# Fewer signals from TensorE, and a tie of POOL's gathers to VectorE's masks, in a graph layer kernel

## The chip, the cores and the metric

One Trainium2 chip, one of its cores. The metric is the device time of one execution in microseconds, lower is better. The engines are TensorE (PE), VectorE (DVE), ScalarE (ACT), GpSimd (POOL) and SyncE (SP), each with its own instruction queue; they are ordered among themselves by counters (semaphores) alone: `then_inc` adds to one when an instruction has ended, `wait_ge` holds an engine until it has a value.

## What is computed

A relational graph layer with attention on 50,000 nodes and 25,000 edges, features 64 wide, 10 relations, `dst` sorted:

```python
proj = jnp.einsum('ni,rio->nro', nfeat, relation_weight)
t_r = proj[src, etype]
h_r = proj[dst, etype]
att = jnp.sum(t_r * jnp.tanh(h_r + efeat), axis=-1)
seg_max = jax.ops.segment_max(att, dst, num_segments=n)
ex = jnp.exp(att - seg_max[dst])
a = ex / jax.ops.segment_sum(ex, dst, num_segments=n)[dst]
h_nb = jax.ops.segment_sum(nfeat[src] * a[:, None], dst, num_segments=n)
out = leaky_relu((nfeat + h_nb) @ res_fc_w.T, 0.01) + leaky_relu(nfeat * h_nb @ res_fc2_w.T, 0.01)
x = _layernorm(x + out)
```

## The kernel before

Edges lie 196 to a partition. They are worked in 25 blocks `s` of 8 columns of 128 edges (the last block has 4). Beside them 49 dense tiles `d` of 1024 nodes get the result for nodes without an edge; blocks -1 to 15 take three tiles each (D0, D1, D2; the last of these blocks only one). The rows of nodes with edges are computed per block and scattered over the dense result at the end.

*POOL* gathers the two end rows of each edge column (`gather`, L443 to L453, 388 indirect DMAs, ring `xsd` of 13 blocks), and then scatters the 196 columns of results (`scatter`, L469 to L477). It runs ahead of the blocks that use the rows, so `pace` (L435 to L441) ties it to the progress of TensorE: `pe_marks` walks TensorE's program and lists, for each signal, how many instructions (a weight load and a matmul are two) TensorE has issued by then. Gather n must wait for the last mark with at most 14.6 n - 250 instructions, scatter n goes on at 13.64 each. An early block has 328 such instructions, a late one 256.

*TensorE*, in each block (L627 to L701): D0's four transposes (`dense_turn`), the edge features into `h_ps` (`add_edges`), scores of the block before (`scores`), D0's product (`dense_y`), then ten quads. A quad is four matmuls (16 instructions in the count of POOL's tie) that add one relation to `t_ps` and `h_ps`. Nine take a mask of VectorE, quad 4 the unmasked copy `xc` of ScalarE. Between the quads stand the steps for block f = s - 2 (two `pair_turn`, behind quads 3 and 4, and four products), D1's turn behind quad 5, D1's product behind quad 6, D2's turn behind quad 7, D2's product behind quad 8; last the transposes of the next block's rows (`turn_in`). Each of these steps ended with a signal. From block f = 14 on (`LATE`) the products are two of one kind (`late_y`) and two of another (`late_linear`).

*ScalarE* copies each turned tile from `tr_ps` to SBUF (`dense_copy` L721, `pair_copy` L785) so that TensorE can go on with it; `tr_ps` is one buffer, so the next turn waits for the copy. It also does the tanh (L710, behind quad 9), the plain copy (L716, behind `turn_in`), relus, squares and the normalised output.

*VectorE* makes the masks `xm` of relation r (`mask`, L989 to L997) in a ring of four, so mask m waits for the quad that read mask m - 4; between the masks it does maxima, sums and layer norm steps. `product` (L1003) needs the tanh, and the next block's mask 0 comes behind it.

*SP* loads node tiles (`load_x`), masks' types (`load_typ`) and edge features (`load_e`, ring of three, freed by `eadd_done`).

## Time and profile before

| | us |
|---|---|
| median of 3 runs | 890.75 |
| lowest, highest of the 3 | 890.29, 2936.04 |
| profiled execution, first to last instruction | 908.0 |
| TensorE busy | 642.8 (71%) |
| VectorE busy | 608.1 (67%) |
| POOL busy | 572.8 (63%) |
| ScalarE busy | 514.2 (57%) |
| granted TensorE clock, mean | 0.844 |

The profiled execution is 17 us longer than the median. Times in the profile are counted from its first instruction. In its rows the bracket behind an instruction gives how long its engine was idle before it and what ended the idle time: "issue" and "remote" mean that no instruction of another engine ended just then.

### The profile page before, as it was taken

The numbers are of one execution on the slowest core, as the hardware profiler recorded it, in microseconds if no ns is written. First come the engines' busy times: TensorE is split into PE (matmuls) and PEld (weight loads), VectorE is DVE, ScalarE is ACT, GpSimd is POOL, SyncE is SP. The second block draws the span as 40 slices with busy tenths as digits, with TensorE's granted clock in tenths as the row PEclk, the third lists the DMA queues.
The fourth block names the chain that finished last, engine by engine and source line by source line (L and its number), as shares of the span: only waits on it lengthen the run. The fifth ranks groups of instructions, "written<-read, shape, count | busy, mean of one in ns | idle before, by whom it ended". The sixth has DMA issues, their size and how long they took to land. (4 is left out here: it accounts for less than half of the span.)

```text
span 908.0 us, 13811 instructions
## 1 busy us (share of the span) xinstructions
PE 642.8 (71%) x3948; PEld 356.0 (39%) x3948; DVE 608.1 (67%) x1094; ACT 514.2 (57%) x1457; POOL 572.8 (63%) x594
## 2 busy tenths in 40 slices
PE   2587778877777877877887876877788778865030
PEld 1434343544443443443443443343344344344020
DVE  2459768778778868869778769865686567754050
ACT  0255575577677667767677677744455244555052
POOL 7466666666666666666666666666666666666726
PEclk9788988798998998999897989879987889786555
DMA  5332432333332432432432421321111110000000
GB/s 139 107 101 71 115 103 81 114 103 81 115 103 81 116 104 69 127 103 67 128 104 60 123 81 45 104 73 64 50 48 43 62 57 28 27 29 28 24 6 17
DMA packets 48035, 70.37 MB, mean 77 GB/s; under 512 B 15971, under 2 KB 19487, under 8 KB 47959
## 3 DMA queue, kind: packets, MB, share of 16 engines
q1 hardware_dynamic: 18562, 32.97, 11.6%
q0 software_dynamic: 18752, 17.29, 9.1%
q10 hardware_dynamic: 10644, 19.23, 5.7%
q8 instruction: 32, 0.52, 0.2%
q14 instruction: 45, 0.36, 0.1%
HBM read 45.60 MB, written 25.78 MB: 79 GB/s over the span
## 5 line engine op out<-in xcount | busy, mean ns | idle before, releaser
L450 POOL DMA_INDIRECT xsd<-in_x,ends_i x388 | 378.4, 975 | 219.4 <-issue 91.1
L558 PE MATMUL t_ps<-xm,w_rel 64*64 64x512 f32 (+1 forms) x900 | 263.1, 682 | 17.7 <-DVE xm L996 9.2
L996 DVE SCALAR_TENSOR_TENSOR xm<-typ,xT_ps 128x1024 f32<-128x1024 f32 (+1 forms) x225 | 264.4, 1185 | 14.6 <-ACT xc L716 9.9
L560 PE MATMUL h_ps<-xm,w_rel 64*64 64x512 f32 (+1 forms) x900 | 264.3, 682 | 0.7 <-issue 0.4
L474 POOL DMA_INDIRECT out<-out_r,row_i x196 | 191.3, 976 | 110.4 <-issue 51.7
L575 PE MATMUL y_ps<-bd_cat,dT 128*128 128x256 f32 x392 | 127.0, 481 | 48.1 <-issue 28.6
L575 PEld LDWEIGHTS y_ps<-bd_cat,dT 128*128 128x128 f32 x392 | 89.3, 239 | 69.6 <-issue 33.8
L558 PEld LDWEIGHTS t_ps<-xm,w_rel 64*64 64x64 f32 x900 | 57.8, 149 | 118.4 <-issue 81.9
L740 ACT ACTIVATE o_t<-zd,rstd 128x64 f32<-128x64 f32 x392 | 98.8, 340 | 0.0
L585 PE MATMUL tr_ps<-ident,uw 128*128 128x128 f32 x196 | 35.9, 312 | 70.3 <-DVE uw L1090 31.9
L1058 DVE TENSOR_TENSOR zd<-rd,y_ps 128x512 f32<-128x512 f32 x49 | 33.4, 681 | 57.5 <-issue 29.8
L585 PEld LDWEIGHTS tr_ps<-ident,uw 128*128 128x128 f32 x196 | 23.3, 155 | 112.0 <-issue 75.9
L785 ACT COPY uwT<-tr_ps 128x512 f32<-128x512 f32 x49 | 28.4, 580 | 67.9 <-PE tr_ps L585 33.6
L1003 DVE TENSOR_TENSOR prod<-t_ps,g_t 128x512 f32<-128x512 f32 (+1 forms) x25 | 17.0, 680 | 71.8 <-issue 42.3
L1038 DVE SCALAR_TENSOR_TENSOR es<-es,wd,wx 128x64 f32<-128x64 f32 x196 | 55.4, 282 | 11.7 <-DVE es L1038 0.5
L595 PEld LDWEIGHTS s_ps<-bd_both,uwT 128*128 128x128 f32 x224 | 32.2, 207 | 75.9 <-issue 70.0
L541 PE MATMUL h_ps<-ident,ea 128*128 128x128 f32 x196 | 31.1, 307 | 41.0 <-issue 24.0
L710 ACT ACTIVATE g_t<-h_ps 128x512 f32<-128x512 f32 (+1 forms) x25 | 14.7, 587 | 80.3 <-remote 77.7
L595 PE MATMUL s_ps<-bd_both,uwT 128*128 128x128 f32 x224 | 43.1, 319 | 23.3 <-issue 23.3
L560 PEld LDWEIGHTS h_ps<-xm,w_rel 64*64 64x64 f32 x900 | 58.0, 149 | 3.5 <-issue 3.5
L726 ACT ACTIVATE rd<-y_ps 128x512 f32<-128x512 f32 x49 | 28.9, 590 | 46.4 <-remote 20.2
L764 ACT ACTIVATE wx<-xsd,wd 128x64 f32<-128x64 f32 x196 | 52.1, 338 | 0.8
(161 smaller groups left out, 982.8 us busy)
## 6 DMA issues: line engine op xcount, KB each, us to landing
x_in<-in_x SPq DMA_DIRECT2D x48, 256.0 KB
typ<-typ_d SPq DMA_DIRECT2D x24, 512.0 KB
out<-o_t ACTq DMA_DIRECT2D x48, 256.0 KB
xsd<-in_x SPq DMA_DIRECT2D x512, 0.2 KB
xsd<-in_x,ends_i POOLq DMA_INDIRECT x388
hist<-es ACTq DMA_DIRECT2D x24, 256.0 KB
ea<-in_edge_attr SPq DMA_DIRECT2D x24, 224.0 KB
out<-out_r,row_i POOLq DMA_INDIRECT x196
```

The costliest lines, as they stand in the source:

```text
L450: pool.indirect_dma_start(xsd[:, s % RX, j, side, :], None, x[:, :], bass.IndirectOffsetOnAxis(ap=ends_i[:, side, c:c + 1], axis=0),).then ...
L474: pool.indirect_dma_start(out[:, :], bass.IndirectOffsetOnAxis(ap=row_i[:, c:c + 1], axis=0), out_r[:, s % RW, j, :], None, bounds_check=t ...
L558: pe.matmul(t_ps[h * D:(h + 1) * D, 0:n], w[0:D, :], moving[0:D, h * n:(h + 1) * n], start=(at == 0), stop=(at == R - 1), skip_group_check ...
L560: mm = pe.matmul(h_ps[(1 - h) * D:(2 - h) * D, 0:n], w[D:P, :], moving[D:P, (1 - h) * n:(2 - h) * n], start=False, stop=(at == R - 1), ski ...
L575: mm = pe.matmul(y_ps[:, j * 2 * P:(j + 1) * 2 * P], dT[:, d % 2, j * P:(j + 1) * P], bd_cat.rearrange("p k f -> p (k f)"), start=True, st ...
L585: mm = pe.transpose(tr_ps[:, j * P:(j + 1) * P], uw[:, g * QUAD + j, :, :].rearrange("p k f -> p (k f)"), ident[:, :])
L595: mm = pe.matmul(s_ps[:, YQ + j * P:YQ + (j + 1) * P], uwT[:, q // 2, k * P:(k + 1) * P], bd_both[:, :], start=True, stop=True)
L740: ins = act.activation(o_t[:, d % RO, j * D:(j + 1) * D], zd[:, d % RZ, j * D:(j + 1) * D], ACT.Copy, scale=rstd[:, s % 2, d % 3, j:j + 1])
L764: ins = act.activation(wx[:, j, :], xsd[:, e % RX, j, 0, :], ACT.Copy, scale=wd[:, e % 2, 0, j:j + 1])
L996: v.scalar_tensor_tensor(xm[:, m % RM, 0:n], typ[:, s % RT, 0:n], float(r), xT_ps[:, 0:n], ALU.is_equal, ALU.mult).then_inc(masked, 1)
L1038: v.scalar_tensor_tensor(es[:, e % RS, j, :], old, wd[:, e % 2, 1, j:j + 1], wx[:, j, :], ALU.mult, ALU.add).then_inc(chain_done, 1)
L1058: v.tensor_tensor(zd[:, d % RZ, :].rearrange("p (j f) -> p j f", j=4), rd[:, d % 2, :].rearrange("p (j f) -> p j f", j=4), y_ps.rearrange( ...
```

## The change

TensorE no longer signals behind the edge features, behind quads 0, 2, 3, 5, 6 and 8, nor behind the first of two products of a kind in a late block. All who waited for these wait for the next signal that is left: masks for quads 1, 4, 7 or 9, the edge load for quad 1. `quads_until(s, at)` gives the count of quad signals that says that quad `at` of block s is done. `pe_marks` is replaced by `mask_marks`: the tie of POOL now reads `masked`, VectorE's count of masks; mask r of a block stands for (r + 1)/9 of the block's TensorE instructions. The constants of the tie stay.

```diff
+    POSTS = [1, PLAIN_AT, 7, R - 1]
+
+    def quads_until(s, at):
+        return len(POSTS) * s + sum(1 for n in POSTS if n < at) + 1
+
+    def mask_read(m):
+        return quads_until(m // RB, m % RB + (1 if m % RB >= PLAIN_AT else 0))
+
+    Q_BEFORE = [0]
+    for s in range(NS):
+        Q_BEFORE.append(Q_BEFORE[-1] + (2 * groups(s) if s < LATE else 2))
...
+        def mask_marks():
+
+            marks, work, ends = [], 0, {}
             for s in range(-1, LAST + 1):
                 main, e, f, d = 0 <= s < NS, s - 1, s - 2, tiles(s)
+                other = 24 * len(d) + (2 * cols(e) if 0 <= e < NS else 0) + (24 * groups(f) if 0 <= f < NS else 0)
+                if main:
+                    other += 2 * cols(s) + R * 16
+                if 0 <= s + 1 < NS:
+                    other += 2 * cols(s + 1)
+                for r in range(RB):
                     if main:
+                        marks.append((masked, s * RB + r + 1, work + other * (r + 1) // RB))
+                work += other
+                ends[s] = work
             return marks, ends
...
-                wait(sp, eadd_done, s - RE + 1)
+                wait(sp, quad_done, quads_until(s - RE, 0) if s >= RE else 0)
...
-            (marks, ends), at = pe_marks(), [-1]
+            (marks, ends), at = mask_marks(), [-1]
...
-                mm.then_inc(eadd_done, 1)
...
-                mm.then_inc(quad_done, 1)
+                if at in POSTS:
+                    mm.then_inc(quad_done, 1)
... (late_y and late_linear alike)
-                mm.then_inc(y12_done, 1)
+                if g == groups(f) - 1:
+                    mm.then_inc(y12_done, 1)
...
-                act.wait_ge(quad_done, (e + 1) * R)
+                act.wait_ge(quad_done, quads_until(e, R - 1))
...
-                wait(act, quad_done, (s - 1) * R + PLAIN_AT + 1 if s > 0 else 0)
+                wait(act, quad_done, quads_until(s - 1, PLAIN_AT) if s > 0 else 0)
...
-                wait(v, quad_done, quad_count(m - RM) if m >= RM else 0)
+                wait(v, quad_done, mask_read(m - RM) if m >= RM else 0)
...
-                v.wait_ge(y12_done, Q_BEFORE[f] + groups(f))
+                v.wait_ge(y12_done, Q_BEFORE[f] + 1)
```

## Rows read from the trace of the kernel before

**Rows 1.** The page, part 1: busy us (share of the span) xinstructions

```profile
PE 642.8 (71%) x3948; PEld 356.0 (39%) x3948; DVE 608.1 (67%) x1094; ACT 514.2 (57%) x1457; POOL 572.8 (63%) x594
```

**Rows 2.** Stretches: us, busy us of PE, PEld, DVE, ACT, POOL, clock, DMA

```profile
50.00:600.00 550.00, 428.79 (x2628) 236.63 (x2620) 423.13 (x720) 373.72 (x1087) 349.16 (x359) 0.89 0.34 97
600.00:825.00 225.00, 174.79 (x1136) 89.85 (x1136) 145.87 (x264) 98.77 (x272) 144.75 (x149) 0.84 0.13 44
825.00:908.00 83.00, 16.43 (x74) 14.29 (x74) 19.78 (x60) 31.42 (x83) 48.75 (x50) 0.52 0.06 19
```

**Rows 3.** Instruction groups of POOL: busy us, mean ns, idle before them

```profile
L450 POOL DMA_INDIRECT xsd<-in_x,ends_i x388 | 378.4, 975 | 219.4 <-issue 91.1 <-remote 69.4 <-PE h_ps L560 26.3
...
L474 POOL DMA_INDIRECT out<-out_r,row_i x196 | 191.3, 976 | 110.4 <-issue 51.7 <-remote 29.2 <-ACT out_r L810 15.6
```

**Rows 4.** Waits over the span: us in total, times, longest

```profile
ACT g_t L710 <- remote: 77.7, 13, 10.4
```

**Rows 5.** Timeline of POOL, block 11: start us, us, instruction, idle before

```profile
421.99 0.95 POOL L450 DMA_INDIRECT xsd<-in_x,ends_i  x1 [1.35 <-remote]
...
429.48 0.95 POOL L450 DMA_INDIRECT xsd<-in_x,ends_i  x1 [1.54 <-remote]
```

**Rows 6.** Timeline of ScalarE, block 11

```profile
421.82 0.59 ACT L785 COPY uwT<-tr_ps 128x512 f32<-128x512 f32 x1 [0.72 <-remote]
...
423.27 0.57 ACT L785 COPY uwT<-tr_ps 128x512 f32<-128x512 f32 x1
...
429.25 0.59 ACT L721 COPY dT<-tr_ps 128x512 f32<-128x512 f32 x1 [2.00 <-remote]
...
441.57 0.60 ACT L710 ACTIVATE g_t<-h_ps 128x512 f32<-128x512 f32 x1 [1.81 <-remote]
```

**Rows 7.** Timeline of TensorE, block 11

```profile
417.98 0.66 PE L585 MATMUL tr_ps<-ident,uw 128*128 128x128 f32 x4 [0.22 <-issue]
...
425.76 1.06 PE L568 MATMUL tr_ps<-ident,x_in 128*128 128x128 f32 x4
...
429.88 1.99 PE L575 MATMUL y_ps<-bd_cat,dT 128*128 128x256 f32 x8 [1.38 <-ACT dT L721]
```

**Rows 8.** Timeline of VectorE, block 11 (L996: masks; L1058: dense add)

```profile
411.73 2.34 DVE L996 SCALAR_TENSOR_TENSOR xm<-typ,xT_ps 128x1024 f32<-128x1024 f32 x2
...
429.11 1.21 DVE L996 SCALAR_TENSOR_TENSOR xm<-typ,xT_ps 128x1024 f32<-128x1024 f32 x1
433.88 0.69 DVE L1058 TENSOR_TENSOR zd<-rd,y_ps 128x512 f32<-128x512 f32 x1 [3.56 <-ACT rd L726]
...
445.91 2.34 DVE L996 SCALAR_TENSOR_TENSOR xm<-typ,xT_ps 128x1024 f32<-128x1024 f32 x2
```

**Rows 9.** Timelines of TensorE, POOL and ScalarE, the kernel's start

```profile
24.09 0.60 PE L568 MATMUL tr_ps<-ident,x_in 128*128 128x128 f32 x4
...
27.89 0.95 POOL L450 DMA_INDIRECT xsd<-in_x,ends_i  x1 [0.31 <-issue]
...
32.66 0.59 ACT L721 COPY dT<-tr_ps 128x512 f32<-128x512 f32 x1 [5.33 <-remote]
```

**Rows 10.** Timelines of TensorE, POOL and VectorE, the tail

```profile
832.33 3.62 PE L606 MATMUL y_ps<-bd_relu,uwT 128*128 128x128 f32 x16
...
837.20 1.00 PE L613 MATMUL tr_ps<-bd_lin,uwT 128*128 128x64 f32 x8
...
825.55 0.97 POOL L474 DMA_INDIRECT out<-out_r,row_i  x1 [1.68 <-remote]
...
861.40 0.97 POOL L474 DMA_INDIRECT out<-out_r,row_i  x1 [0.31 <-issue]
877.98 0.97 POOL L474 DMA_INDIRECT out<-out_r,row_i  x1 [15.61 <-ACT out_r L810]
...
844.05 0.69 DVE L1111 SCALAR_TENSOR_TENSOR zf<-y_ps,xsd 128x512 f32<-128x512 f32 x1 [6.16 <-remote]
...
866.60 0.69 DVE L1122 TENSOR_TENSOR zf<-zf,tr_ps 128x512 f32<-128x512 f32 x1 [21.13 <-remote]
```

More of the change, by code:

```diff
@@ L64, in gnn_resnorm @@
         G_BEFORE.append(G_BEFORE[-1] + groups(s))
-    Q_BEFORE = [2 * n for n in G_BEFORE]
     C_BEFORE = [QUAD * n for n in G_BEFORE]
@@ L82, in gnn_resnorm @@
     PLAIN_AT = 4
-    def quad_count(m):
-        return m // RB * R + m % RB + (2 if m % RB >= PLAIN_AT else 1)
+    POSTS = [1, PLAIN_AT, 7, R - 1]
[3 more added lines that the diff above has]
+        return quads_until(m // RB, m % RB + (1 if m % RB >= PLAIN_AT else 0))
     LATE = (ND - 1) // 3 - 2
+    Q_BEFORE = [0]
+    for s in range(NS):
+        Q_BEFORE.append(Q_BEFORE[-1] + (2 * groups(s) if s < LATE else 2))
     ROW_BLOCKS = [8, 13, 19, 24]
@@ L214, in gnn_resnorm @@
         scattered = sems("scattered", RW)
-        xT_done, masked, quad_done, eadd_done = sem("xT_done"), sem("masked"), sem("quad_done"), sem("eadd_done")
+        xT_done, masked, quad_done = sem("xT_done"), sem("masked"), sem("quad_done")
         tanh_done, prod_done, att_done, max_done = sem("tanh_done"), sem("prod_done"), sem("att_done"), sem("max_done")
@@ L540, in add_edges @@
                 for i in range(half):
-                    mm = pe.matmul(h_ps[:, i * P:(i + 1) * P], ea[:, s % RE, 2 * i:2 * i + 2, :].rearrange("p h f -> p (h f)"),
+                    pe.matmul(h_ps[:, i * P:(i + 1) * P], ea[:, s % RE, 2 * i:2 * i + 2, :].rearrange("p h f -> p (h f)"),
                                    ident[:, :], start=(i == 0), stop=False, skip_group_check=True)
-                mm.then_inc(eadd_done, 1)
             def quad(s, at):
@@ L613, in late_linear @@
                     mm = pe.matmul(tr_ps[:, j * D:(j + 1) * D], uwT[:, g, k * P:(k + 1) * P], bd_lin[:, :], start=True, stop=True)
-                mm.then_inc(y12_done, 1)
+                if g == groups(f) - 1:
+                    mm.then_inc(y12_done, 1)
             def pair_part(f, q):
```

46 lines of the change are left out of this document (removed).

## The prediction

> **What bounds the kernel now.** I read the page first: the span, the busy times, the two big groups of POOL. No engine is full: over the span TensorE, the busiest, is busy 71% [rows 1]. The stretch table says where: from 50 to 600 us TensorE has 428.8 us of work in 550, from 600 to 825 us 174.8 in 225, and from 825 us on almost none, at half clock [rows 2]. So in 25 blocks TensorE waits about a fifth of the time, and then there is a tail. I looked for the waits by name next. The costliest idle with an unseen cause is ScalarE's ahead of the tanh: 77.7 us in 13 cases, put down to "remote" [rows 4]. The tanh waits for one TensorE signal, that of quad 9.
>
> Then one block (s = 11) in time, engine by engine, signal against waiter. The first pair turn ends at 417.98 + 0.66 = 418.64; its copy on ScalarE starts at 421.82, 3.2 us later, 0.72 us of it with ScalarE idle [rows 7, 6]. D1's turn ends at 425.76 + 1.06 = 426.82; its copy starts at 429.25, 2.4 us later, after 2.00 us of idle [rows 7, 6]. Yet the second pair turn, which can't begin before the first copy ends at 421.82 + 0.59 = 422.41, is copied at 423.27: at once [rows 6]. What differs is POOL. Its indirect DMAs come back to back, 0.30 us apart, in runs of four to six, with breaks of 1.35 and 1.54 us that end at 421.99 and 429.48: 0.17 and 0.23 us behind the two late copies [rows 5, 6]. So POOL, which also waits for TensorE's signals, got them at the same moment. My reading is that a TensorE signal sent inside a run is read when the run has stopped.
>
> The two places where a run is long bear this out. At the start POOL issues 20 gathers in a row, the last at 27.89. D1's first turn ends at 24.09 + 0.60 = 24.69 and is copied at 32.66: 8.0 us late, 3.8 us after POOL fell still at 27.89 + 0.95 [rows 9]. In the tail 29 indirect DMAs run from 825.55 to 862.37. The relu products end at 832.33 + 3.62 = 835.95 and VectorE takes them at 844.05, 8.1 us late; the linear ones end at 838.20 and are taken at 866.60, 28.4 us late, 4.2 us after POOL's last [rows 10]. So what bounds the kernel is the chain of TensorE and ScalarE steps, stretched by TensorE signals that wait out POOL's runs, and at the end 20 scatters of 1.28 us from 877.98 on, behind that chain [rows 3, 10].
>
> The Trainium skill, page "Perfetto Trace Analysis", section "Per-engine timelines", says that the end of a matmul in a profile is an estimate of the profiler and the signal comes after the write is acknowledged. This case agrees that lateness of tenths may be the estimate; 8.0 and 28.4 us can't be.
>
> **The change part by part.** *Signals.* An early block (three dense tiles) signals 25 times: ten quads, one each for edges, scores and x turns, six for the dense tiles, two pair turns, four products. Six quads and the edges go: 18. A late block goes from 19 to 10. No matmul gets shorter or starts sooner by itself, so I cost the removal at 0 on TensorE. What it may save is queueing in front of the signals that matter, which is the rival below.
>
> *Coarser waits.* Masks 4, 6 and 8 now wait for quads 1, 4 and 7 in place of 0, 2 and 5. Quads 1 and 4 are long done. Mask 8 started at 429.11 [rows 8], while quad 7 comes behind D1's product, 429.88 + 1.99 = 431.87, and takes about 1 us: the mask starts some 4 us later and ends at about 434.2 [rows 7, 8]. Queued behind it on VectorE is D1's add, which ScalarE's relu held until 433.88 anyway [rows 8]; it slips by 0.3 us, and by as much as quad 7's signal is late. TensorE needs it only for D2's product, behind quad 8 and two more products. I cost it at 0 and keep 1 us a block as its bound. The edge load now waits for quad 1 of a block two back: 0. The plain copy and the tanh wait for the same quads as before.
>
> *The tie.* This is the part with weight. Before, POOL's gather n waits for TensorE's work to reach 14.6 n - 250 instructions, in 20-odd marks a block, and those marks are themselves the signals that come late: the tie stops POOL after some five gathers, and the stop lets the signals out. Now the marks are the nine masks. An early block is 72 + 16 + 48 + 176 + 16 = 328 instructions, so a mask frees 36.4/14.6 = 2.5 gathers and a block 22.5. One gather costs 0.95 + 0.30 = 1.25 us [rows 3, 5], so 2.5 of them 3.1 us. The masks start at 411.73 to 429.11, eight steps in 17.4 us (2.2 us each) [rows 8]: faster than POOL works them off. So POOL will run from mask 0 without a stop: masks 0 to 5 need only quad 1, and free 15 gathers, 18.8 us; all nine are 28 us. Then it rests until the next mask 0 (445.91, so this period is 34.2 us [rows 8]). A late block is 256 instructions: 18.8 scatters of 1.28 us, 24 us out of 28.
>
> What sits inside the run: the two pair turns and D1's turn, each of which TensorE must get back through a ScalarE copy. Each is now late by 0 to 3.2 us, about 2.8 where it is late. Inside a long run the rows give 8.0 and 8.1 us. So the step per signal is bounded by -2.8 (prompt) and +5.2 (as in the long runs). I take +1.6, nearer to the steady rows: the first of the three still falls in the first 6 us of the run. Early block: 3 x 1.6 = +4.8. At the boundary POOL rests, so quad 9's signal comes sooner; of the 1.81 us idle before the tanh [rows 6] I give back 1.2, as the end of a 28 us run and the 4 us behind it reach to +32. Net +3.6, times 16 = +58 us. Late block: two signals, +3.2, nothing at the boundary, since a run of 24 us fills it; times 9 = +29 us.
>
> *Head.* Masks start only with block 0, and the first frees gather 25 or 26: (88 + 29 + 250)/14.6 = 25.1. POOL issues 26 gathers in place of 20 before it stops, 6 x 1.25 = +7.5 us, and D1's turn, which waits out that run, is as much later. *Tail.* The last mask is done before the last quads, so POOL starts its last run earlier, and three signals stand in it in place of five. The waits there are 6.16 and 21.13 us [rows 10]; the run's length doesn't change, only its start, by some 6 scatters: -8 us.
>
> Sum: 58 + 29 + 7.5 - 8 = +86 on the profiled 908.0 us: 994 us. The median of the runs is 890.75, 0.981 of the profiled execution; 994 x 0.981 = **975 us**.
>
> **Rivals.** (1) *Fewer signals, faster.* If TensorE's signals leave one by one through gaps in a run, those that matter pass sooner when 7 of 25 others are gone, and the boundary, where tanh, plain copy and scores hang one behind the other, falls into POOL's rest. For it: not every signal is late, as the second pair turn shows [rows 6]. Against: that one came 1.2 us into a run (421.99), not deep in one [rows 5]. Price: 1.8 us in each of 25 blocks, 45 us, head and tail cancelling: 863, as a median 846; with 28% off each of three late signals (0.8 us x 3 x 16 = 38 us more) 810. It decides if the second pair turn is copied within 3 us inside a run of more than ten. Chance 0.30, some of it (0.03) too small to tell.
> (2) *No effect.* The lateness may hang on something else than POOL's run length, and the tie still sets POOL's mean rate of 22.5 gathers a block: same period, 891 us. Against: both long runs. Chance 0.13. The Trainium skill, page "VectorE: DVE Perf Modes", section "The DRAIN you can't avoid", measured that a semaphore behind each of eight copies costs nothing over one behind the last; carried to TensorE it gives this rival's time. The trace agrees as far as TensorE's own work goes, and disagrees for the waiters.
> (3) *Full starvation.* The signals wait out the whole run. Then the second pair copy comes 18.8 + 4 = 22.8 us after mask 0's end in place of 10.3 (423.27 against 411.73 + 1.2): 12.5 x 16 = 200, and half of it in 9 late blocks, 56: 908 + 256 = 1164 profiled, 1142. Against: masks 6 and 8 hang on quads 4 and 7, so POOL starves itself sooner. Chance 0.10.
> My forecast has 0.47, with 915 to 1050 as its own range.
>
> **Numbers.** A measurement of this kernel can tell 2% from no change. Faster by more: 0.27, from (1). Within 2%: 0.17, from (2), 0.03 of (1) and the low end of mine. Slower: 0.56. The range of 830 to 1060 leaves out the far part of (1), about 0.09, and (3) with the top of mine, about 0.11.
>
> **What would show it.** In the profile after: POOL in runs of 15 or more from mask 0, then a rest of 5 us or more ahead of the next mask 0; the second pair copy over 10 us behind mask 0; periods of 36 to 40 us for 34.2; the tanh's idle shorter. Runs of POOL still of five would show the tie wrong; long runs with prompt copies would show (1). The head's copy at about 40 us in place of 32.66 tests the mechanism by itself. The prediction fails if lateness falls with the number of signals more than it grows with the run.

## The result and the profile after

| | us |
|---|---|
| changed kernel, median of 4 runs | 1091.24 (1080.38 to 1094.78) |
| kernel before, median | 890.79 |
| ratio, 95% interval | 1.2233, 1.2178 to 1.2288 |
| profiled execution of the changed kernel, first to last instruction | 1078.7 (before: 908.0) |

The change costs 22%. Slower was the forecast, but 975 us was far too low, and the range to 1060 us did not hold the time.

The work itself is the same. Part 1 of the page (busy us, share of the span, instructions) of the changed kernel, against [rows 1]:

```profile
PE 649.4 (60%) x3948; PEld 351.7 (33%) x3948; DVE 607.9 (56%) x1094; ACT 515.0 (48%) x1457; POOL 577.5 (54%) x594
```

TensorE is busy 6.6 us longer (649.4 against 642.8; its mean granted clock was 0.785 against 0.844) and no other engine by more than 5 us; nearly all of the 170.7 us between the two spans is waiting. Where it was lost shows in the start of a block's mask 0. Timelines of VectorE, first of the kernel before and then of the changed one, masks 0 of blocks 0, 16 and 24 (a row can hold several masks):

```profile
42.67 3.48 DVE L996 SCALAR_TENSOR_TENSOR xm<-typ,xT_ps 128x1024 f32<-128x1024 f32 x3
...
577.30 2.35 DVE L996 SCALAR_TENSOR_TENSOR xm<-typ,xT_ps 128x1024 f32<-128x1024 f32 x2 [1.13 <-ACT xc L716]
...
801.45 1.28 DVE L996 SCALAR_TENSOR_TENSOR xm<-typ,xT_ps 128x512 f32<-128x512 f32 x2
```

```profile
50.13 3.48 DVE L964 SCALAR_TENSOR_TENSOR xm<-typ,xT_ps 128x1024 f32<-128x1024 f32 x3
...
725.86 2.34 DVE L964 SCALAR_TENSOR_TENSOR xm<-typ,xT_ps 128x1024 f32<-128x1024 f32 x2
...
983.19 1.28 DVE L964 SCALAR_TENSOR_TENSOR xm<-typ,xT_ps 128x512 f32<-128x512 f32 x2 [0.16 <-ACT xc L684]
```

| part | before | after | difference | forecast |
|---|---|---|---|---|
| head, to mask 0 of block 0 | 42.7 | 50.1 | +7.5 | +7.5 |
| 16 early blocks | 534.6 | 675.7 | +141.1 | +58 |
| 8 of the late blocks | 224.2 | 257.3 | +33.2 | +29 for nine |
| last block and tail | 106.6 | 95.5 | -11.0 | -8 |

Half of the loss stands in the forecast; what is missing is nearly all in the early blocks. The waits of the changed kernel (us in total, times, longest) name it. In the kernel before the longest entry with an unseen cause was the tanh's 77.7 us [rows 4]; now it is the copy of the pair turns, then the masks that wait for TensorE, and POOL, which waits for masks:

```profile
ACT uwT L753 <- remote: 264.6, 37, 13.3
POOL xsd L416 <- DVE xm L964: 258.1, 63, 15.8
DVE xm L964 <- remote: 180.8, 25, 10.9
```

One early block of the changed kernel (s = 9), timelines of POOL, TensorE, ScalarE and VectorE. L416 are the gathers, L525 the last matmul of quad 4, L551 the pair turns, L753 their copies, L678 the tanh, L964 the masks:

```profile
431.47 0.94 POOL L416 DMA_INDIRECT xsd<-in_x,ends_i  x1 [5.16 <-DVE xm L964]
...
451.66 0.94 POOL L416 DMA_INDIRECT xsd<-in_x,ends_i  x1 [0.30 <-issue]
458.52 1.24 POOL L416 DMA_INDIRECT xsd<-in_x,ends_i  x1 [5.91 <-DVE xm L964]
...
464.41 1.35 POOL L416 DMA_INDIRECT xsd<-in_x,ends_i  x1 [0.31 <-issue]
473.04 0.94 POOL L416 DMA_INDIRECT xsd<-in_x,ends_i  x1 [7.29 <-DVE xm L964]
...
437.29 0.59 PE L525 MATMUL h_ps<-xc,w_rel 64*64 64x512 f32 x1
439.94 0.63 PE L551 MATMUL tr_ps<-ident,uw 128*128 128x128 f32 x4 [2.06 <-issue]
...
439.23 0.56 ACT L753 COPY uwT<-tr_ps 128x512 f32<-128x512 f32 x1
...
454.06 0.58 ACT L753 COPY uwT<-tr_ps 128x512 f32<-128x512 f32 x1 [13.30 <-remote]
...
467.19 0.59 ACT L678 ACTIVATE g_t<-h_ps 128x512 f32<-128x512 f32 x1
...
429.99 2.34 DVE L964 SCALAR_TENSOR_TENSOR xm<-typ,xT_ps 128x1024 f32<-128x1024 f32 x2
...
447.09 1.22 DVE L964 SCALAR_TENSOR_TENSOR xm<-typ,xT_ps 128x1024 f32<-128x1024 f32 x1 [4.51 <-remote]
...
471.56 2.34 DVE L964 SCALAR_TENSOR_TENSOR xm<-typ,xT_ps 128x1024 f32<-128x1024 f32 x2
```

POOL issues 17 gathers back to back from 431.47 to 452.60, rests 5.91 us, does five more by 465.76 and rests 7.29 us. The second pair turn ends at 440.57 and is copied at 454.06, 13.5 us late, 1.5 us after the run's end. Mask 0 ended at about 431.2, so the copy comes 22.9 us behind it, where it came 10.3 us behind it in block 11 of the kernel before. From this copy to the tanh it takes 13.1 us where it took 18.3 (423.27 to 441.57, [rows 6]). 12.6 lost, 5.2 given back: this is the 7.4 us by which the period is longer (471.56 - 429.99 = 41.6; 34.2 in block 11 before).

The first pair turn, 5.4 us into the run, was not held (its copy at 439.23 waited only for ScalarE); quad 4 ends at 437.88 (it signals), and the mask that needs it starts at 447.09, 9.2 us later but 5.5 us before the run ends. So a held signal can come out inside a run. In block 3 it is the first pair turn's. Its two copies and POOL's last gather of the run that began at 175.93:

```profile
189.45 0.58 ACT L753 COPY uwT<-tr_ps 128x512 f32<-128x512 f32 x1 [7.56 <-remote]
...
197.25 0.59 ACT L753 COPY uwT<-tr_ps 128x512 f32<-128x512 f32 x1 [6.26 <-remote]
...
193.63 0.94 POOL L416 DMA_INDIRECT xsd<-in_x,ends_i  x1 [0.30 <-issue]
```

The first turn ends at 181.74 and is copied 7.7 us later, inside the run; the second can only then begin, ends at 191.26 and is copied 6.0 us later, 2.7 us after the run's end. Over blocks 2 to 15 the second copy comes 21.3 us behind mask 0's end (11.5 before), and from there to the next mask 0 it takes 20.1 us (21.4 before): 9.8 us lost, 1.3 given back. The 5.2 us of blocks 9 and 11 are not typical.

Head and tail of the changed kernel: POOL, ScalarE (L689: copy of a dense tile) and VectorE (L1079: takes the relu products):

```profile
34.88 0.94 POOL L416 DMA_INDIRECT xsd<-in_x,ends_i  x1 [0.30 <-issue]
51.62 0.94 POOL L416 DMA_INDIRECT xsd<-in_x,ends_i  x1 [15.81 <-DVE xm L964]
...
40.15 0.58 ACT L689 COPY dT<-tr_ps 128x512 f32<-128x512 f32 x1 [5.71 <-remote]
...
1029.47 0.97 POOL L440 DMA_INDIRECT out<-out_r,row_i  x1 [0.30 <-issue]
...
1033.39 0.69 DVE L1079 SCALAR_TENSOR_TENSOR zf<-y_ps,xsd 128x512 f32<-128x512 f32 x1 [6.72 <-remote]
```

26 gathers in place of 20, and D1's first copy at 40.15 in place of 32.66 [rows 9], 7.5 us later: as forecast. In the tail a run of 20 scatters (1005 to 1030, ahead of the last scatters, which start at 1037) holds the relu products until 1033.39, and the wait of 21.13 us behind them [rows 10] is gone.

### The profile page after: what moved, and what is told of

The parts are those of the page before. It is cut to its first block and busy times, and to the rows that moved or that the text cites. A ratio compares the mean times of both kernels' runs of the same rounds, so it can differ in the third digit from the quotient of the medians.

```text
span 1078.7 us, 13797 instructions
## 1 busy us (share of the span) xinstructions
PE 649.4 (60%) x3948; PEld 351.7 (33%) x3948; DVE 607.9 (56%) x1094; ACT 515.0 (48%) x1457; POOL 577.5 (54%) x594
## 5 line engine op out<-in xcount | busy, mean ns | idle before, releaser
L416 POOL DMA_INDIRECT xsd<-in_x,ends_i x388 | 382.6, 986 | 363.3 <-DVE xm L964 258.1
L964 DVE SCALAR_TENSOR_TENSOR xm<-typ,xT_ps 128x1024 f32<-128x1024 f32 (+1 forms) x225 | 264.5, 1186 | 285.8 <-remote 180.8
L523 PE MATMUL t_ps<-xm,w_rel 64*64 64x512 f32 (+1 forms) x900 | 276.6, 704 | 18.0 <-DVE xm L964 14.5
L525 PE MATMUL h_ps<-xm,w_rel 64*64 64x512 f32 (+1 forms) x900 | 276.6, 704 | 0.0
L753 ACT COPY uwT<-tr_ps 128x512 f32<-128x512 f32 x49 | 28.6, 583 | 269.8 <-remote 264.6
L541 PE MATMUL y_ps<-bd_cat,dT 128*128 128x256 f32 x392 | 113.1, 440 | 62.3 <-ACT dT L689 49.2
L551 PE MATMUL tr_ps<-ident,uw 128*128 128x128 f32 x196 | 41.0, 346 | 148.6 <-issue 105.5
L541 PEld LDWEIGHTS y_ps<-bd_cat,dT 128*128 128x128 f32 x392 | 83.5, 224 | 80.0 <-ACT dT L689 55.8
L534 PE MATMUL tr_ps<-ident,x_in 128*128 128x128 f32 x196 | 36.6, 319 | 105.4 <-issue 61.9
L551 PEld LDWEIGHTS tr_ps<-ident,uw 128*128 128x128 f32 x196 | 26.6, 172 | 188.8 <-issue 169.1
L561 PE MATMUL s_ps<-bd_both,uwT 128*128 128x128 f32 x224 | 49.3, 354 | 28.4 <-issue 28.4
L534 PEld LDWEIGHTS tr_ps<-ident,x_in 128*128 128x128 f32 x196 | 26.7, 164 | 112.1 <-issue 111.8
L1006 DVE SCALAR_TENSOR_TENSOR es<-es,wd,wx 128x64 f32<-128x64 f32 x196 | 55.1, 281 | 12.5 <-ACT wx L732 1.3
L1048 DVE RECIPROCAL rstd<-sd 128x32 f32<-128x32 f32 x29 | 10.2, 352 | 77.4 <-ACT sd L765 49.2
L525 PEld LDWEIGHTS h_ps<-xm,w_rel 64*64 64x64 f32 x900 | 53.0, 149 | 0.0
L778 ACT ACTIVATE out_r<-zcf,rstd 128x64 f32<-128x64 f32 x196 | 49.1, 333 | 0.0
L689 ACT COPY dT<-tr_ps 128x512 f32<-128x512 f32 x49 | 28.8, 588 | 39.6 <-remote 36.8
```

What stands on the lines that cost most here:

```text
L416: pool.indirect_dma_start(xsd[:, s % RX, j, side, :], None, x[:, :], bass.IndirectOffsetOnAxis(ap=ends_i[:, side, c:c + 1], axis=0),).then ...
L523: pe.matmul(t_ps[h * D:(h + 1) * D, 0:n], w[0:D, :], moving[0:D, h * n:(h + 1) * n], start=(at == 0), stop=(at == R - 1), skip_group_check ...
L525: mm = pe.matmul(h_ps[(1 - h) * D:(2 - h) * D, 0:n], w[D:P, :], moving[D:P, (1 - h) * n:(2 - h) * n], start=False, stop=(at == R - 1), ski ...
L534: mm = pe.transpose(tr_ps[:, j * P:(j + 1) * P], x_in[:, d % RI, j * P:(j + 1) * P], ident[:, :])
L541: mm = pe.matmul(y_ps[:, j * 2 * P:(j + 1) * 2 * P], dT[:, d % 2, j * P:(j + 1) * P], bd_cat.rearrange("p k f -> p (k f)"), start=True, st ...
L551: mm = pe.transpose(tr_ps[:, j * P:(j + 1) * P], uw[:, g * QUAD + j, :, :].rearrange("p k f -> p (k f)"), ident[:, :])
```

## The experiments

The theory: a signal of TensorE that is sent while POOL issues indirect DMAs back to back is read when the run has stopped (by block 3 above that can't be the whole rule); the mask tie makes the runs long; the fewer signals and the coarser waits cost nothing. Rivals: the coarser waits or the missing signals bring the loss; the number of signals matters; POOL's run has nothing to do with it.

### One part of the change alone, and the first surprise

tie_only has all signals of the kernel before and the new tie; signals_only the reverse; mask_tie_pair_stops is the changed kernel with two more stops of POOL; head_26 is the kernel before with a longer first run.

```diff
tie_only, against the kernel before:
-            (marks, ends), at = pe_marks(), [-1]
+            (marks, ends), at = mask_marks(), [-1]
signals_only, against the changed kernel (pe_marks without the signals that are gone):
-            (marks, ends), at = mask_marks(), [-1]
+            (marks, ends), at = pe_marks(), [-1]
mask_tie_pair_stops, in mask_marks (and POOL waits for every mark that it passes):
+                        if r == 2 and 0 <= f < NS:
+                            marks.append((tr_out, TR_PAIR[f, 0] + 1, work + other * (r + 1) // RB))
+                        if r == 3 and 0 <= f < NS:
+                            marks.append((tr_out, TR_PAIR[f, 1] + 1, work + other * (r + 1) // RB))
head_26, in pace of the kernel before:
+                if n < 26:
+                    return
```

tie_only:


> All of TensorE's signals as in the kernel before; only POOL's tie is the new one (it reads VectorE's masks). Theory (a TensorE signal sent while POOL issues indirect DMAs back to back is read when the run stops, and the tie makes the runs long): nearly the whole loss is here, 1050 to 1110 us, POOL in runs of 15 gathers from mask 0, second pair copy about 22 us behind mask 0. If the loss came from the signals taken away or from the coarser mask waits: 880 to 905 us.

signals_only:


> The signals taken away and the coarser waits as in the changed kernel; POOL's tie still reads TensorE, by the marks that are left (12 to 15 a block in place of 25). Theory: the runs of POOL grow little, so little is lost: 885 to 915 us, late waits of 2 to 4 us as before. If fewer signals or the coarser waits were the cause of the loss: above 1000 us. If fewer signals help (my rival 1 of the prediction): 810 to 875 us.

mask_tie_pair_stops:


> The changed kernel, but POOL also stops within its run, at the third mask for ScalarE's copy of the block's first pair turn and at the fourth for that of its second. Nothing else differs. Theory: each stop lets TensorE's signal out, so both pair copies come within 4 us of the turn, the second 10 to 14 us behind mask 0 in place of 20 to 23, and most of the 141 us lost in the early blocks comes back: 930 to 990 us. If long runs in themselves (or the tie's rate, or coarser mask waits) are the cause: 1060 us or more, since an added wait of POOL can only delay it.

head_26:


> The kernel before; only POOL's first 26 gathers are free of the tie, in place of 20. Theory: ScalarE's copy of the second dense tile, which waits out the first run, comes 6 x 1.25 = 7.5 us later, and block 0's first mask too: 898 us, 0.8% above before. If the copy waits for something else than POOL's run: 891 us, copy at 32.7 us as before.

Measured: 765.85, 764.60, 765.34 and 765.25 us, beside a kernel before of **766.05 us** (31 runs, 762.57 to 767.64). Ratios 0.9996 [0.9978, 1.0013], 0.9990 [0.9975, 1.0005], 1.0001 [0.9985, 1.0017], 0.9992 [0.9971, 1.0014]. Every number of these expectations was missed, because the kernel before itself was 125 us faster than at first (890.79). The page of tie_only, its two groups of POOL (busy us, mean ns, idle before them), and two rows of POOL's timeline:

```profile
L408 POOL DMA_INDIRECT xsd<-in_x,ends_i x388 | 383.6, 989 | 119.2 <-issue 108.0
...
L432 POOL DMA_INDIRECT out<-out_r,row_i x196 | 193.5, 987 | 59.7 <-issue 58.8
...
405.67 0.99 POOL L408 DMA_INDIRECT xsd<-in_x,ends_i  x1 [0.30 <-issue]
406.96 0.95 POOL L408 DMA_INDIRECT xsd<-in_x,ends_i  x1 [0.30 <-issue]
```

POOL issues its 584 indirect DMAs without one pause over 0.6 us from the first to the last: 383.6 + 119.2 + 193.5 + 59.7 = 756 of 764.4 us. Here TensorE's signals are read at once in the middle of an endless run: the second pair copy starts within 0.2 us of its turn in every block. So the sum of my prediction rests on a condition that is not always there. Without it POOL is the bound, the tie never stops it, and neither part of the change matters.

### Is it the program, or the condition it runs in?

after_again is the changed kernel, before_again the one before, both unedited; head_26_again is head_26. more_signals is the kernel before with two signals more behind each quad's inner matmuls:

```diff
                 for h in range(2):
                     pe.matmul(t_ps[h * D:(h + 1) * D, 0:n], w[0:D, :], moving[0:D, h * n:(h + 1) * n],
-                              start=(at == 0), stop=(at == R - 1), skip_group_check=True)
+                              start=(at == 0), stop=(at == R - 1), skip_group_check=True).then_inc(extra, 1)
```

after_again:


> The changed kernel as it is, measured again, because four variants and the kernel before itself all took 765 us together where the kernel before had taken 891 earlier. Two readings: (a) what made TensorE's signals late is no part of the program but of the chip or its condition, and where the kernel before takes 766 us the changed kernel takes 760 to 775 too, bound by POOL's 584 indirect DMAs of 1.25 us (730 us) back to back; where the kernel before takes 890, the changed one takes 1080 to 1095. (b) The change itself brings the lateness in any condition: 950 us or more beside a kernel before of 766.

before_again:


> The kernel before, for a profile of it beside the others. Reading (a): about 766 us, POOL without breaks from 3.5 us on, D1's first copy at about 25 us in place of 32.7; if the late signals are back, 891 us and 32.7 us.

head_26_again:


> The kernel before with the first 26 gathers free, once more. If signals are late here: about 898 us, D1's first copy at about 40 us. If they are prompt: 766 us, copy at about 25 us.

more_signals:


> The kernel before with two more signals of TensorE behind each quad's inner matmuls, which nobody reads (20 more a block, 45 in place of 25). If signals are late here and they leave one by one through gaps (my rival 1): each of the three late signals of a block has up to twice as many ahead, 3 x 1.6 x 25 = 120 us more, about 1000. If they all leave when POOL's run stops: within 1% of the kernel before. If signals are prompt: equal to the kernel before, 766 us.

Measured, together: kernel before 900.79 us (13 runs, 896.18 to 912.49), after_again 1071.61, ratio 1.1879 [1.1777, 1.1981]; before_again 898.75; head_26_again 914.09; more_signals 909.24, ratio 1.0058 [1.0011, 1.0105]. The late signals were back, and reading (a) holds: the same programs come in two conditions (the changed kernel a little under the 1080 to 1095 that I had expected). The whole series:

| measured together | record's chip number | kernel before |
|---|---|---|
| tie_only, signals_only, mask_tie_pair_stops, head_26 | 8 | 766 |
| after_again, before_again, head_26_again, more_signals | 2 | 901, late |
| tie_only_2, signals_only_2, pair_stops_2, tie_handoffs | 9 | 765 |
| probes_mixed; all_mixed | 5; 13 | 763; 768 |
| all_mixed_b | 2 | 763 |
| all_mixed_c | 9 | 910, late |
| loaded_probes; loaded_probes_b | 8; 14 | 766; 765 |

Numbers 2 and 9 show both, so it isn't fixed to a chip's number; inside one group it never changed. The profile tells which it is by the span of the kernel before and by POOL's runs.

The head tests the mechanism. Timelines of ScalarE, before_again and then head_26_again with POOL's last gather of the first run (ScalarE: L726 and L728 D0's relu, L721 and L723 the copy of D1; both kernels' turn of D1 ends at 25.1):

```profile
30.39 0.60 ACT L726 ACTIVATE rd<-y_ps 128x512 f32<-128x512 f32 x1 [9.98 <-remote]
31.15 0.59 ACT L721 COPY dT<-tr_ps 128x512 f32<-128x512 f32 x1 [0.16 <-remote]
```

```profile
30.46 0.60 ACT L728 ACTIVATE rd<-y_ps 128x512 f32<-128x512 f32 x1 [10.03 <-remote]
38.86 0.59 ACT L723 COPY dT<-tr_ps 128x512 f32<-128x512 f32 x1 [7.80 <-remote]
...
35.59 0.94 POOL L452 DMA_INDIRECT xsd<-in_x,ends_i  x1 [0.30 <-issue]
```

Nothing but POOL's tie differs, seven gathers more (26 against 19 in before_again) move D1's copy by 7.7 us, and 914.09 is 1.7% above 898.75 (one run of each; I had said 0.8%). The time by itself proves little: the slowest of the 13 runs of the kernel before took 912.49. But the relu, whose product ended at about 24.3, starts at 30.4 in both, in head_26_again 6 us before the run ends. So "read when the run has stopped" is not exact: inside a run a held signal can still come out, here some 6 us late; only the next one waited for the run's end. The first profile of the kernel before had this too: there the same product ends at 24.26 and its relu starts at 26.73, inside the run that ends at 28.84. Twenty more signals a block (more_signals) cost 0.6%, so a queue of signals has little weight while runs are short: that is against my rival 1.

The traces also record each rise of a counter, and there the signal itself is late, not its reading: the turns' counter in block 9 above rises at 454.04, 0.02 us ahead of the copy. Counted over the changed kernel's first profile, with a run as indirect DMAs less than 0.6 us apart, TensorE's counters rise within 0.4 us of the matmul's end for 74 of the 89 signals in the first 3 us of a run, 11 of 53 from 3 to 6 us, 5 of 73 later in a run, and 157 of 168 outside of runs. Some 20 of these 383 signals have no record at all, too few to explain it. In tie_only, with POOL in one endless run, it is 571 of 578.

### The same experiments again, and a tie on the hand-overs

tie_handoffs has the changed kernel's signals, and its marks are ScalarE's copies and relus, the masks, the tanh and the plain copy, each at TensorE's place in the program:

```diff
+                def turned(k):
+                    if len(d) > k:
+                        mark(tr_out, TR_DENSE[d[k]] + 1, 8)
+                def multiplied(k):
+                    if len(d) > k:
+                        mark(relu_done, d[k] + 1, 16)
```

tie_only_2:


> Again all of TensorE's signals and only the tie new, since one chip reads signals promptly and others late. Where the kernel before takes about 890 to 900 us: theory (long runs of POOL's indirect DMAs hold the signals) 1040 to 1110 us, runs of 15 from mask 0; signals or coarser mask waits as the cause: 885 to 915. Where the kernel before takes 766: 766.

signals_only_2:


> Again the fewer signals and coarser waits with POOL's tie on TensorE. Where the kernel before takes about 890 to 900 us: theory 885 to 930 (the marks that are left are farther apart, so runs grow a little, the head's from 20 to 26 as in the changed kernel); fewer signals as a gain: 810 to 875; coarser waits or fewer signals as the loss: above 1000. Where the kernel before takes 766: 766.

pair_stops_2:


> Again the changed kernel with two more stops in POOL's run, for ScalarE's copies of the two pair turns. Where the kernel before takes about 890 to 900 us and the changed one 1070 to 1090: theory, a stop lets the signals out, both copies within 4 us of their turns and 100 us or more won back, 930 to 990; if a stop of POOL doesn't matter, 1060 or more. Where the kernel before takes 766: 766.

tie_handoffs:


> The changed kernel's fewer signals, but POOL's tie reads the answers to TensorE's signals instead of masks alone: ScalarE's copies of each turned tile, its relus, its tanh and plain copy, and the masks, each at TensorE's place in the program. POOL so stops until each hand-over has been taken, in 20-odd marks a block. Theory: every late signal finds POOL at rest soon after it is sent, 860 to 900 us where the kernel before takes 890 to 900. If the stops cost POOL more than they give (its 584 DMAs need 730 us of any span): 920 or more. Where the kernel before takes 766: 766 to 775.

Measured: kernel before 764.98, and 764.53, 763.49, 762.55, 764.51 us; ratios 0.9991 [0.9978, 1.0003], 0.9981 [0.9971, 0.9991], 0.9974 [0.9961, 0.9987], 0.9989 [0.9977, 1.0000]. No late signals, so only the last sentence of each expectation was put to the test, and it held. The 0.2 and 0.3% of fewer signals did not show in the first series (0.9990, 1.0001): I make nothing of them.

### Every treatment in one execution

Because a whole kernel may meet the wrong condition, the next kernels change their treatment from block to block, and stand behind small probes of the signal itself. A probe is eight rounds between a sender and an answerer beside one kind of work on POOL.

```diff
+            lists = [f() for f in (pe_marks, mask_marks, stop_marks, act_marks)]
+            for s in range(-1, LAST + 1):
+                kind = next((k for a, b, k in kinds if a <= s <= b), 0)
+                marks += [m[:3] for m in lists[kind][0] if m[3] == s]
...
+    def posts(s):
+        return range(R) if s in FULL else POSTS
... (TensorE's side of a probe)
+                        wait(engine, pong, m)
+                        engine.transpose(tr_ps[:, 0:P], ident[:, :], ident[:, :]).then_inc(ping, 1)
... (ScalarE's side)
+                        engine.wait_ge(ping, m + 1)
+                        engine.copy(dT[:, 0, 0:P], tr_ps[:, 0:P]).then_inc(pong, 1)
```

probes_mixed:


> Ahead of the kernel stand seven probes, and then the kernel before runs (all of TensorE's signals) with POOL's tie by blocks: on TensorE's marks to block 4 and from block 17, on the masks in blocks 5 to 10, on the masks with the two stops for the pair copies in blocks 11 to 16. A probe: a sender does one small operation and signals, an answerer copies and signals back, eight times, while POOL (1) rests, (2, 3, 4, 7) issues 16 gathers of 1.25 us, (5) does 16 memsets, (6) issues 16 direct DMAs. Senders and answerers: TensorE and ScalarE in 1, 2, 5, 6 and 7 (7: each gather waits for the one before to land), VectorE and ScalarE in 3, TensorE and VectorE in 4. On a chip where the kernel before takes about 890 us I expect: 1 and 3 in under 8 us; 2 and 4 not done before the run of gathers is (over 20 us); 5 as 1; 6 not known, 7 at the gathers' own pace, about 2 us a round. If TensorE's signals are late for another reason, 2 is as fast as 1. The blocks: before's period of some 33 us in blocks 1 to 4, 40 to 43 in 6 to 10 if the long run is the cause (33 if not), 33 to 37 in 12 to 16 if stops let signals out. On a chip where the kernel before takes 766 us: all probes under 10 us (7 too), and all blocks equal at about 27 us.

all_mixed:


> The same seven probes, and behind them a kernel whose blocks differ. Blocks 1 to 5: all of TensorE's quad signals, POOL's tie on the masks. Blocks 6 to 9: the changed kernel's fewer signals and coarser waits, tie on TensorE's marks that are left. Blocks 10 to 12: fewer signals, tie on the masks, with the two stops for the pair copies. Blocks 13 to 16 and 21 to 24: fewer signals, tie on the hand-overs (ScalarE's copies and relus, masks). Blocks 17 to 20: as 6 to 9. On a chip with late signals I expect: probes 1 and 3 in under 8 us, 2 and 4 not before POOL's run ends (over 20 us), 5 as 1; blocks 2 to 5 at 40 to 44 us (the tie is the cause; about 34 if the signals were), blocks 7 to 9 at 33 to 36 (about 42 if fewer signals or coarser waits were), blocks 11 and 12 at 33 to 37, blocks 14 to 16 at 31 to 34. On a chip where the kernel before takes 766 us: the seven probes as fast as one another and all early blocks at about 27 us.

all_mixed_b:


> The kernel whose blocks differ, once more (blocks 1 to 5: all quad signals, tie on the masks; 6 to 9 and 17 to 20: fewer signals, tie on TensorE's marks; 10 to 12: fewer signals, tie on the masks with the two stops; 13 to 16 and 21 to 24: fewer signals, tie on the hand-overs), behind nine probes: the seven of before, and two more of TensorE and ScalarE in which POOL issues 16 gathers in fours, resting behind each four until they have landed (8), or doing two memsets of 0.47 us behind each four (9). On a chip with late signals: probes 1 and 3 under 8 us, 2 and 4 not before POOL's run ends (over 20 us), 5 as 1, 8 one to three rounds in each rest, 9 like 8 if it is the issue of DMAs that holds the signals and like 2 if it is POOL being busy. Blocks 2 to 5 at 40 to 44 us, 7 to 9 at 33 to 36, 11 and 12 at 33 to 37, 14 to 16 at 31 to 34. On a chip where the kernel before takes 766 us: all probes alike and all early blocks at about 27 us, as two runs have shown.

all_mixed_c:


> The same kernel as the last, on whichever chip it meets. With late signals (kernel before about 890 us): probes 1 and 3 under 8 us, 2 and 4 over 20 us, 5 as 1; blocks 2 to 5 at 40 to 44 us, 7 to 9 at 33 to 36, 11 and 12 at 33 to 37, 14 to 16 at 31 to 34. Without: probes alike, early blocks about 27 us.

probes_mixed, all_mixed and all_mixed_b met no late signals: spans of 918.7, 920.5 and 966.2 us with the probes in them, and for instance all of all_mixed's periods from block 2 to block 14 between 27.3 and 28.6 us, whatever the treatment. all_mixed_c met them (kernel before 909.96, this kernel 1218.01).

*The blocks.* VectorE's timeline of all_mixed_c, masks 0 of blocks 2, 6, 10, 11 and 13, and below it those of blocks 2 and 6 in before_again and in after_again:

```profile
312.18 2.34 DVE L1199 SCALAR_TENSOR_TENSOR xm<-typ,xT_ps 128x1024 f32<-128x1024 f32 x2
...
494.61 2.34 DVE L1199 SCALAR_TENSOR_TENSOR xm<-typ,xT_ps 128x1024 f32<-128x1024 f32 x2
...
631.61 2.34 DVE L1199 SCALAR_TENSOR_TENSOR xm<-typ,xT_ps 128x1024 f32<-128x1024 f32 x2
...
682.46 2.34 DVE L1199 SCALAR_TENSOR_TENSOR xm<-typ,xT_ps 128x1024 f32<-128x1024 f32 x2
...
768.84 2.34 DVE L1199 SCALAR_TENSOR_TENSOR xm<-typ,xT_ps 128x1024 f32<-128x1024 f32 x2
```

```profile
98.46 2.34 DVE L996 SCALAR_TENSOR_TENSOR xm<-typ,xT_ps 128x1024 f32<-128x1024 f32 x2
...
236.26 2.34 DVE L996 SCALAR_TENSOR_TENSOR xm<-typ,xT_ps 128x1024 f32<-128x1024 f32 x2
```

```profile
125.01 2.34 DVE L964 SCALAR_TENSOR_TENSOR xm<-typ,xT_ps 128x1024 f32<-128x1024 f32 x2
...
300.48 2.34 DVE L964 SCALAR_TENSOR_TENSOR xm<-typ,xT_ps 128x1024 f32<-128x1024 f32 x2
```

| blocks of all_mixed_c | signals, tie | period | same blocks, kernel before | same blocks, changed kernel |
|---|---|---|---|---|
| 2 to 5 | all of the quads, masks | 45.6 | 34.5 | 43.9 |
| 6 to 9 | fewer, TensorE | 34.3 | 34.0 | 41.5 |
| 11, 12 | fewer, masks with stops | 43.2 | 35.2 | 43.0 |
| 14 to 16 | fewer, hand-overs | 34.4 | 30.3 | 36.5 |
| 17 to 20 | fewer, TensorE | 28.9 | 27.6 | 32.8 |
| 21 to 23 | fewer, hand-overs | 30.4 | 28.1 | 31.7 |

(Periods in us, each the distance between two mask-0 rows over the number of blocks; the two right-hand columns from before_again and after_again. I had expected 40 to 44, 33 to 36, 33 to 37 and 31 to 34 in the first four rows.) The tie alone brings the whole loss of an early block, 11.1 us, and a bit more than the changed kernel's 9.4. The fewer signals with their coarser waits cost 0.3 us in early blocks and 1.3 us in late ones, inside what one block differs from another (32.7 to 35.9 us in blocks 6 to 9). Both halves of my theory on the change stand, in the one execution that could test them. The hand-over tie is no gain: 2 to 4 us a block behind the kernel before.

The stops are a miss: 33 to 37 us expected, 43.2 measured, though they did what they should. ScalarE's timeline of all_mixed_c, block 11, with POOL's two runs (L987 pair copy, L992 takes a pair product, L928 D1's relu):

```profile
691.71 0.56 ACT L987 COPY uwT<-tr_ps 128x512 f32<-128x512 f32 x1
...
693.14 0.56 ACT L987 COPY uwT<-tr_ps 128x512 f32<-128x512 f32 x1
...
704.48 0.37 ACT L992 COPY l<-s_ps 128x256 f32<-128x256 f32 x1 [4.97 <-remote]
...
714.44 0.60 ACT L928 ACTIVATE rd<-y_ps 128x512 f32<-128x512 f32 x1 [8.37 <-remote]
...
693.04 0.94 POOL L620 DMA_INDIRECT xsd<-in_x,ends_i  x1 [2.35 <-ACT uwT L987]
...
710.50 0.94 POOL L620 DMA_INDIRECT xsd<-in_x,ends_i  x1 [0.30 <-issue]
716.52 0.95 POOL L620 DMA_INDIRECT xsd<-in_x,ends_i  x1 [5.08 <-DVE xm L1199]
```

The second pair copy comes at 693.14, 0.1 us behind its turn. Then POOL makes up for the stop with 15 gathers in a row, and the stall moves to the next signals: the second product of the pairs (ended at 697.89, taken at 704.48, inside the run) and D1's product, ended at 699.65 and read at 714.44, 14.8 us late and 3.0 us after the run's end. What counts is not which signal a stop serves, but how long the run behind it is.

*The probes.* One round of probe 2 in all_mixed_c, beside POOL's run (L463 TensorE's transpose, L471 ScalarE's copy, L643 the gathers):

```profile
31.46 0.47 PE L463 MATMUL tr_ps<-ident 128*128 128x128 f32 x1 [0.35 <-ACT dT L471]
31.97 0.27 ACT L471 COPY dT<-tr_ps 128x128 f32<-128x128 f32 x1 [0.56 <-issue]
32.13 0.94 POOL L643 DMA_INDIRECT out_r<-in_x,ends_i  x1 [0.30 <-issue]
```

I expected over 20 us for the eight rounds of probes 2 and 4. The eighth copy starts 6.4 and 6.6 us in, a round each 0.83 us, in the same execution whose blocks lose 10 us each to late signals. So a run of gathers alone does not hold TensorE's signals in its first 6.4 us, though in the kernel most are held from about 3 us on (11 of 53 in time, above). Every probe was prompt, which leaves the probes unable to tell gathers from memsets or direct DMAs.

### Longer and loaded probes

A round here may hold eight matmuls like those of two quads, probes run beside 24 gathers (30 us), and VectorE and SP can be given work.

```diff
+        PROBES = [(0, 0, ""), (24, 0, ""), (0, 2, ""), (24, 2, ""), (24, 0, "v"), (24, 0, "sp"), (24, 2, "v sp"), (4, 2, ""),
+                  (24, 2, "signals"), (24, 2, "v sp signals")]
+        ROUNDS, OPS, LOADS = [26, 26, 10, 10, 26, 26, 10, 10, 10, 10], 30, 12
```

loaded_probes (the first eight of them):


> On a chip with late signals the first probes came out prompt, which fells the simple form of my theory: eight rounds between TensorE and ScalarE took 6.4 us beside a run of gathers, as without one. They covered only the first 6.4 us of the run, and nothing else ran. Here eight probes, ahead of the kernel with fewer signals and the tie on TensorE (signals_only). A round: TensorE (optionally after eight matmuls like those of two quads) transposes and signals, ScalarE copies and signals back. (1) 26 rounds, POOL at rest; (2) 26 rounds beside 24 gathers in one run; (3) 10 loaded rounds, POOL at rest; (4) 10 loaded rounds beside the run; (5) as 2 with VectorE adding without a pause; (6) as 2 with 12 direct DMAs of 256 KB issued by SP; (7) as 4 with both; (8) as 4, POOL resting behind every four gathers. On a chip with late signals: theory A (the run fills something after some 3 us, whatever else goes on) 2 to 7 all stall until the run ends, 30 us; theory B (it takes traffic of other DMAs beside the gathers) only 6 and 7; theory C (it takes TensorE's own load) 4 and 7, and 8 in part; theory D (VectorE's load) 5 and 7. The kernel behind: blocks as in the kernel before, within 1 us of its periods. Without late signals: 2, 5 and 6 as 1, and 4, 7 and 8 as 3.

loaded_probes_b:


> The eight probes of the last run and two more: (9) as 4, with four more signals of TensorE in each round that nobody reads; (10) as 7, with those signals too. On a chip with late signals: theory A (length of the run alone) 2 and 4 to 7, 9 and 10 all stall to the run's end at about 30 us; B (other DMA traffic) 6, 7 and 10; C (TensorE's load) 4, 7, 9 and 10; D (VectorE's load) 5, 7 and 10; E (many signals of TensorE close together) 9 and 10 only. The kernel behind it (fewer signals, tie on TensorE's marks): periods as in the kernel before, 33 to 36 us in blocks 2 to 14. Without late signals: 4, 7, 8, 9 and 10 end within 3 us of 3, and 2, 5 and 6 as 1.

Both met no late signals (kernel before 766.13 and 764.93). Probes 2, 5 and 6 took 21.7 us (1: 23.0), and 4, 7, 8, 9 and 10 25.7 to 29.7 (3: 27.4), each copy 0.04 us behind its transpose: what I expected for this condition, and inconclusive on the question. Theories A to E were not told apart.

## Why the prediction was wrong, and where it was right

*What bounds the kernel.* Right, with a limit I did not know. TensorE's signals are late in POOL's runs: the head moved by 7.5 us in the changed kernel and by 7.7 in head_26_again. But it is a condition that was absent in most of my measurements.

*Signals and coarser waits at 0.* Right: 0.3 us in an early block of all_mixed_c, within my bound of 1 us; the late blocks' 1.3 us lies over it, but within what one block differs from another. My list of masks left some out: mask 7 now waits for quad 4 in place of 3, and the next block's masks 0 and 2 for quads 7 and 9 in place of 6 and 8.

*The tie: shape of the runs.* Right: runs of 15 or more from mask 0, a rest ahead of the next mask 0. *Head and tail.* +7.5 and -11.0 against +7.5 and -8. The head came as worked out. The tail's number is partly luck: I had the run ahead of the last scatters keep its length and start sooner; it shrank from 29 scatters to 20, and the last one grew from 20 to 29.

*The step that failed* is the price of a signal inside a run, "I take +1.6, nearer to the steady rows", times three. It took an average of lateness over signals, with the two long runs (8.0 and 8.1 us) as the upper end. Measured over blocks 2 to 15, from the end of the turn to its copy: first pair turn 2.4 us before and 4.6 after, second 1.1 and 9.3, D1's 2.1 and 3.7. That is 5.6 and 17.6 us a block, +12.0 where I had +4.8. The turns hang on one another through `tr_ps`, and inside a long run that chain gets through at most one stall: either the second turn alone waits for the run's end (block 9: 13.5 us, far above my upper end), or the first comes out inside the run and the second waits for the end (block 3: 7.7 and 6.0), and in blocks 4, 11 and 14 D1's turn is the one that waits last. D1's is mostly prompt, since by then the run is over. So the term had to be priced by the end of the run, at 9.8 us for the second copy. The 1.2 us that I gave back were about right (1.3). Over 16 blocks it made +141.1 and not +58 us. Late blocks, with runs of 12 or 13, came out at 4.2 us each (33.2 / 8) against the 3.2 I had.

*Rivals.* (3) had the step nearly right, the second copy 22.8 us behind mask 0 against 22.9 in block 9 and 21.3 on the mean. But it counted from block 11's 10.3 us, where the mean was 11.5, and took nothing back (12.5 a block; the mean was 8.8). The truth lay between my own sum and that rival, and I gave this stretch too little: its middle, 1060 to 1142 us, is where the time fell. (1) would have needed prompt copies in long runs; with late signals they waited. Its picture of signals that leave one by one is borne out in part: the counters rise in the order in which the signals were sent, in block 9 at 447.07, 454.04 and 455.54. (2), no effect, was wrong here but for a reason it did not name it is true in the other condition, as far as was run: all variants are within 0.3% of the kernel before there, but the changed kernel as it stands was not among them. The Trainium skill, page "VectorE: DVE Perf Modes", section "The DRAIN you can't avoid", says that a semaphore behind each of eight VectorE copies costs nothing over one behind the last; the runs come close to it for TensorE (0.3 us a block for seven signals fewer, 0.6%, interval 0.1 to 1.05%, for twenty more).

*What would show it.* Of what I had listed, the runs of 15, the rests, the copy over 10 us behind mask 0, the head's copy at 40 us (40.15) and the shorter idle of the tanh came; but the copy's 10 us were no test, since block 11 of the kernel before had 10.3 already. The periods of 36 to 40 us did not: from block 2 to 14 they are 40.9 to 46.5.

*What stays open.* What holds the signals. In the condition where they are late, they are late only in or just after runs of POOL (13.5 us late beside a run, prompt in a rest), and more gathers in a run make it worse, with nothing else changed. Yet a bare run did not hold them in its first 6.4 us, and in the head D0's first turn, 15 us into the first run, was copied at once (its copy's preparation starts at 18.53 in before_again, 0.1 us behind the turn). So the run is needed but is not enough. Whether TensorE's or VectorE's load, other transfers or many signals close together must be added was not settled, nor what brings the condition on. One rival was not tested at all, that the recording of the profile has a part in it. In the late condition the traces lack records of the counters that VectorE and ScalarE raise (151 for 225 masks and 57 for ScalarE's 98 copies of turned tiles in before_again), and in the prompt one hardly any (224 and 97 in tie_only). Nothing faster than the kernel before was found for either condition.

## What to carry to other kernels

A tie that paces one engine by another also sets how long its bursts are. Size it by the longest burst it allows, not by its mean rate, and put the marks where the burst can be broken just behind each hand-over that others wait for; a stop that is followed by a longer burst only moves the stall. When a step is one of "a signal waits for the rest of a run", follow the chain of hand-overs to the run's end, not one signal at a time, and then ask what the waiting gives back, over many blocks and not in one pair of them. And measure the kernel before in the same series as the change: here it took 766 or 900 us, and the change cost 19 to 22% in the second case, while its variants made no difference in the first.

## What the runs showed of the hardware

- The same program on the same kind of chip took 763 to 768 us in one condition and 890 to 912 us in another; a series of runs kept to one. In the prompt condition an engine that waits for TensorE's signal reads it within about 0.1 us of the end of the matmul, beside an unbroken run of 584 indirect DMAs; in the late one up to 14.8 us later.
- In the late condition held signals come out after the run's end (1.5 us behind POOL's last indirect DMA in block 9 of the changed kernel, 2.7 in its block 3, 3.0 in block 11 of all_mixed_c, 4.3 in the changed kernel's head), or singly inside a run, 2.5 to 9.4 us late (26.73 in the first profile of the kernel before, 30.46 in head_26_again, 704.48 in all_mixed_c, 447.09 in the changed kernel, and 33.84 in its head, for a product that ended at 24.45). Signals sent in a run's first 3 us were mostly prompt (74 of 89), later ones mostly not (16 of 126). Signals of ScalarE and VectorE were not seen late, though many of their records are missing there: a probe of VectorE and ScalarE, and TensorE's next transpose behind each of ScalarE's copies in the probes (0.35 us idle), were prompt throughout.
- An indirect DMA costs POOL 1.25 us in either condition (0.95 and 0.30 us), so 584 of them bound this kernel at some 756 us when nothing else does.
